# A post-norm decoder layer: the first four batches' rows are split before they are turned, and turned by DMA

## The reference, cut to what matters

```python
x = _layernorm(x + attn(x, Wq, bq, Wk, bk, Wv, bv, Wo, bo))          # first norm
x = _layernorm(x + xattn(x, ctx, ctx, mask, wq, wk, wv, wo))         # second
x = _layernorm(x + ffn(x, gate, up, down))                           # third
# _layernorm(x) = (x - mean) / sqrt(var + 1e-5), over the 512 columns
```

## Time and profile before

| | |
|---|---|
| median of three runs | 850.03 us |
| the profiled execution's own time | 849.92 us |
| its span, first to last instruction | 848.1 us |
| TensorE (PE) busy | 827.7 us, 98% |
| VectorE (DVE) busy | 689.2 us, 81% |
| GpSimd (POOL) busy | 632.8 us, 75% |
| ScalarE (ACT) busy | 533.6 us, 63% |
| mean granted TensorE clock | 0.999 of full |

### The profile page before, as it was taken

One profiled execution on the slowest core, in us unless ns is written; L12 is line 12 of the kernel. 1 busy time (PEld: TensorE's weight loads), 2 busy tenths in 40 slices (PEclk: granted clock), 3 DMA queues, 4 the chain that ended last, 5 costly groups with the idle time before them and its releaser, 6 DMA issues.

```text
span 848.1 us, 17377 instructions
## 1 busy us (share of the span) xinstructions
PE 827.7 (98%) x6125; PEld 465.5 (55%) x6125; DVE 689.2 (81%) x1077; ACT 533.6 (63%) x1560; POOL 632.8 (75%) x563
## 2 busy tenths in 40 slices
PE   9899999999999999999999999999999999999997
PEld 4677777655555554555555555555555644434444
DVE  5688788998688778689788788798889755899897
ACT  5798888554765666576575676665666753777400
POOL 1199999897676686578777677578888633999896
PEclk9999999999999999999999999999999999999999
DMA  7675255103244422434425125213442223230011
GB/s 192 194 256 181 63 160 163 54 18 108 38 95 130 112 39 75 112 39 138 105 38 155 33 40 161 38 26 91 133 93 39 46 42 105 72 110 20 2 48 52
DMA packets 120038, 76.76 MB, mean 91 GB/s; under 512 B 72877, under 2 KB 104336, under 8 KB 119952
## 3 DMA queue, kind: packets, MB, share of 16 engines
q1 hardware_dynamic: 117504, 74.86, 33.5%
q10 hardware_dynamic: 2448, 0.79, 0.5%
HBM read 52.50 MB, written 6.36 MB: 69 GB/s over the span
## 4 chain that ended last, share of the span: by engine, by line
PE 62%; POOL 14%; DVE 7%; ACT 7%; issue 6%; DMA 3%; SPq 0%; POOLq 0%; ACTq 0%; DVEq 0%
PE bank L356 16%; PE bank L358 16%; PE bank L357 16%; POOL rot L647 2%; POOL left L680 2%; PE bank L1667 2%; POOL q2l L653 2%; POOL pn L664 2%; ACT prob L845 2%; POOL prob L657 2%; PE bank L1840 1%; PE bank L1841 1%; PE bank L1760 1%; PE bank L1759 1%; PE bank L1758 1%
## 5 line engine op out<-in xcount | busy, mean ns | idle before, releaser
L657 POOL TENSOR_TENSOR prob<-prob,rden 128x512 f32<-128x512 f32 x64 | 67.8, 1060 | 103.3 <-DVE rden L1318 103.0
L647 POOL TENSOR_TENSOR rot<-rcos,rsin 128x512 f32<-128x512 f32 x80 | 106.5, 1332 | 20.3 <-DVE rsin L1260 19.8
L356 PE MATMUL bank<-aTh,xqh 128*128 128x512 f16 x256 | 97.1, 379 | 1.4 <-DVE rsin L1260 0.9
L356 PE MATMUL bank<-xoh,o2h 128*128 128x512 f16 x256 | 97.1, 379 | 0.1
L357 PE MATMUL bank<-xol,o2h 128*128 128x512 f16 x256 | 97.2, 379 | 0.0
L358 PE MATMUL bank<-xoh,o2l 128*128 128x512 f16 x256 | 97.1, 379 | 0.0
L357 PE MATMUL bank<-aTl,xqh 128*128 128x512 f16 x256 | 97.1, 379 | 0.0
L358 PE MATMUL bank<-aTh,xql 128*128 128x512 f16 x256 | 97.1, 379 | 0.0
L1010 ACT ACTIVATE prob<-bank,ebias 128x128 f32<-128x128 f32 x256 | 90.4, 365 | 2.1
L1260 DVE SCALAR_TENSOR_TENSOR rsin<-bank,sinq 64x512 f32<-64x512 f32 x128 | 88.1, 688 | 1.7
L664 POOL TENSOR_TENSOR pn<-prob,pn 128x512 f16<-128x512 f32 x64 | 84.1, 1315 | 6.8 <-ACT pn L1022 6.6
(11 more groups left out here) (224 smaller groups left out, 2652.7 us busy)
## 6 DMA issues: line engine op xcount, KB each, us to landing
tst<-tables SPq DMA_DIRECT2D x11, 768.0 KB, 5.2
xqs<-in_xwq SPq DMA_DIRECT2D x8, 1024.0 KB, 6.6
xos<-in_xwo SPq DMA_DIRECT2D x8, 1024.0 KB, 5.6
qst<-in_fq SPq DMA_DIRECT2D x11, 384.0 KB, 3.4
kstk<-stack SPq DMA_DIRECT2D x48, 64.0 KB, 2.3
qstk<-stack SPq DMA_DIRECT2D x21, 128.0 KB, 2.6
xs<-in_ctxT SPq DMA_DIRECT2D x2, 1024.0 KB, 6.3
res<-in_x SPq DMA_DIRECT2D x1, 2048.0 KB, 8.4
```

The source lines that it names most:

```text
L356: pe.matmul(out_ap, ah, bh, start=first, stop=False)
L647: nc.gpsimd.tensor_tensor(rot[:, r % 2, :], rcos[:, r % 2, :], rsin[:, r % 2, :], ALU.add).then_inc(rope_rot, 1)
L657: nc.gpsimd.tensor_tensor(prob[:, v % 2, :].rearrange("p (h k) -> p h k", h=QH), prob[:, v % 2, :].rearrange("p (h k) -> p h k", h=QH), rd ...
```

## The change

```diff
--- before.py
+++ after.py
@@ -64,9 +64,8 @@
 
 
 
-    plan = [(STEPS1 - 12, "k", (0,)), (STEPS1 - 11, "o", (0,)), (STEPS1 - 10, "o", (1,)), (STEPS1 - 9, "t", (0, 0))]
-    plan += [(STEPS1 - 9, "o", (2,)), (STEPS1 - 8, "t", (0, 1)), (STEPS1 - 8, "o", (3,)), (STEPS1 - 7, "t", (0, 2))]
-    plan += [(STEPS1 - 7, "v", (0,)), (STEPS1 - 6, "t", (0, 3))]
+    plan = [(STEPS1 - 12 + b, "o", (b,)) for b in range(BH)]
+    plan += [(STEPS1 - 8, "v", (0,)), (STEPS1 - 7, "k", (0,))]
     plan += [(STEPS1 - 5 + h, "q", (0, h)) for h in range(QH)]
     plan += [(STEPS1 - 1, "k", (1,)), (STEPS1, "v", (1,))]
     plan += [(STEPS1 + 1, "q", (1, 0)), (STEPS1 + 2, "q", (1, 1)), (STEPS1 + 3, "q", (1, 2)), (STEPS1 + 5, "q", (1, 3))]
@@ -146,7 +145,7 @@
 
 APPLY_SLOT = {(0, b): FILLS[find_fill("o", b)][0] + 1 for b in range(NB)}
 APPLY_SLOT.update({(1, b): T0 + BH * (BLOCK_OF[(G - 1, b // BH)]) + b % BH + 5 for b in range(NB)})
-SHIFTED = [(0, b) for b in range(BH, NB)]
+SHIFTED = [(0, b) for b in range(NB)]
 LATE_TURN = {APPLY_SLOT[(1, b)] + 1: b for b in range(BH, NB)}
 
 
@@ -229,7 +228,7 @@
         lnmv = sb("lnmv", [P, 3, 2], F32)
         lnve, lnrs = sb("lnve", [P, 3, 1], F32), sb("lnrs", [P, 3, 1], F32)
         power = sb("power", [P, 1], F32)
-        lnsh = sb("lnsh", [P, BH, 1], F32)
+        lnsh = sb("lnsh", [P, NB, 1], F32)
         scol16 = sb("scol16", [P, (NI - NSPLIT) * 2 * NK], F16)
         scol = sb("scol", [P, NI - NSPLIT, 2, NK], F32)
 
@@ -281,6 +280,9 @@
         o2h, o2l = at(20, "o2h", [P, 2, QH, S], F16), at(22, "o2l", [P, 2, QH, S], F16)
 
 
+        rows = at(155.5, "rows", [P, 3, 2, D], F16)
+
+
         qst = at(24, "qst", [P, 2, 3 * D], U16)
         tst = at(30, "tst", [P, 2, 2, 3 * D], F16)
         nib = at(42, "nib", [P, 3 * D], U16)
@@ -325,6 +327,7 @@
         oT_hi, oT_lo = sem("oT_hi"), sem("oT_lo")
         ln_sum, ln_stat, ln_aggr, ln_ve, ln_rs, ln_out = (
             sem("ln_sum"), sem("ln_stat"), sem("ln_aggr"), sem("ln_ve"), sem("ln_rs"), sem("ln_out"))
+        rows_hi, rows_lo, rows_in = sem("rows_hi"), sem("rows_lo"), [sem(f"rows_in{i}") for i in range(3)]
         ln_shift, ln_mid, ln_right = sem("ln_shift"), sem("ln_mid"), sem("ln_right")
         xt_hi, late_psum, late_hi, late_lo = sem("xt_hi"), sem("late_psum"), sem("late_hi"), sem("late_lo")
 
@@ -449,6 +452,13 @@
                 else:
                     sp.wait_ge(xo_lo, 4 * g)
                 sp.dma_start(xos[:, :, :], xwo.rearrange("(h p) n -> p h n", p=P)[:, g * QH:(g + 1) * QH, :]).then_inc(xo_in, 16)
+
+            def turn_rows(b):
+                if b == 0:
+                    sp.wait_ge(v1_psum, BLOCKS)
+                for i, (dst, done) in enumerate(((aTh, rows_hi), (aTl, rows_lo))):
+                    sp.wait_ge(done, b + 1)
+                    sp.dma_start_transpose(dst[:, :, b * S:(b + 1) * S], rows[:, b % 3, i, :]).then_inc(rows_in[b % 3], 16)
 
             def turn_probabilities(v):
                 sp.wait_ge(c_pn_lo, v + 1)
@@ -528,6 +538,8 @@
             load_q(1)
             stack_rows(7)
             load_kv(1)
+            for b in range(BH):
+                turn_rows(b)
             load_o(1)
             for t in range(STEPS1 - 8, END + 1):
                 if 1 <= t - T0:
@@ -723,7 +735,7 @@
 
             def inverse_sds(layer, t):
                 for (norm, b), slot in APPLY_SLOT.items():
-                    if norm == layer and slot == t + 1 and (norm, b) not in SHIFTED:
+                    if norm == layer and slot == t + 1 and (layer == 1 or slot < T0):
                         inverse_sd(layer * NB + b)
 
             for t in range(FIRST, END + 7):
@@ -833,6 +845,14 @@
                                      proj_bank(j, "v")[:, :].rearrange("p (b h d) -> p b h d", b=BH, h=HC),
                                      ACT.Copy, scale=2.0 ** (E_V1 - E_X - E_W)).then_inc(v1_hi, 1)
 
+            def split_rows_hi(b):
+                act.wait_ge(ln_out, b + 1)
+                if b == 0:
+                    act.wait_ge(v1_psum, BLOCKS - 1)
+                if b >= 3:
+                    act.wait_ge(rows_in[b % 3], 32 * (b // 3))
+                split_hi(rows[:, b % 3, 0, :], res[:, b, :], E_X).then_inc(rows_hi, 1)
+
             def exps1(u):
                 act.wait_ge(nmax_done, u + 1)
                 if u >= 2:
@@ -960,6 +980,12 @@
             for i, e in enumerate((E_QK, E_QK, E_V1)):
                 split_hi(bcols[:, i, :], bcol[:, i, :], e).then_inc(scaled_bias, 1)
             w1_split_hi(0, 2)
+            def scaled_norm(layer, b):
+                e, r = layer * NB + b, res[:, b, :]
+                act.wait_ge(ln_shift, SHIFTED.index((layer, b)) + 1)
+                nc.scalar.activation(r, r, ACT.Identity, scale=lnrs[:, e % 3, :],
+                                     bias=lnsh[:, SHIFTED.index((layer, b)), :]).then_inc(ln_out, 1)
+
             for t in range(FIRST, T0):
                 j, n = t // TILES1, t % TILES1
                 if j + 1 < BLOCKS and n == 4 and t > -TILES1:
@@ -971,6 +997,10 @@
                     seed_mask(t - STEPS1 + 2)
                 if 1 <= t <= STEPS1:
                     p1_hi(t - 1)
+                for layer, b in SHIFTED:
+                    if APPLY_SLOT[(layer, b)] == t:
+                        scaled_norm(layer, b)
+                        split_rows_hi(b)
                 if j + 2 < BLOCKS and n == 6:
                     k1_out_f32(j + 2)
                 if t == FIRST + 3:
@@ -992,12 +1022,6 @@
                 weight_pieces(t)
                 bank_splits([f for f in fills_at(t) if f not in turned_first(t)])
                 rotations(fills_at(t - 1))
-
-            def scaled_norm(layer, b):
-                e, r = layer * NB + b, res[:, b, :]
-                act.wait_ge(ln_shift, SHIFTED.index((layer, b)) + 1)
-                nc.scalar.activation(r, r, ACT.Identity, scale=lnrs[:, e % 3, :],
-                                     bias=lnsh[:, SHIFTED.index((layer, b)), :]).then_inc(ln_out, 1)
 
             def exps(v):
                 act.wait_ge(c_nmax, v + 1)
@@ -1238,6 +1262,10 @@
                 split_lo(aTl[:, :, b * S:(b + 1) * S], by_k(bank[f % 2][:, :]), aTh[:, :, b * S:(b + 1) * S],
                          E_X).then_inc(fill_free, 1)
 
+            def split_rows_lo(b):
+                dve.wait_ge(rows_hi, b + 1)
+                split_lo(rows[:, b % 3, 1, :], res[:, b, :], rows[:, b % 3, 0, :], E_X).then_inc(rows_lo, 1)
+
             def late_turned_lo(b):
                 dve.wait_ge(late_hi, b - BH + 1)
                 split_lo(aTl[:, :, b * S:(b + 1) * S], by_k(bank[4 + b % 2][:, :]), aTh[:, :, b * S:(b + 1) * S],
@@ -1457,6 +1485,9 @@
                     dve.wait_ge(table_in, 112)
                     nc.vector.tensor_scalar(mbias[:, :, :], mask_f[:, :, :], 0.0, NEG, ALU.is_equal,
                                             ALU.mult).then_inc(mask_ready, 1)
+                for b in range(BH):
+                    if APPLY_SLOT[(0, b)] == t:
+                        split_rows_lo(b)
                 weight_pieces(t - 1)
                 for f in fills_at(t):
                     if f not in turned_first(t):
@@ -1708,7 +1739,11 @@
                     if kind == "k" and n == 0:
                         pe.wait_ge(cT_lo, NHALF * NK)
                 if kind == "q":
-                    pe.wait_ge(fill_free, find_fill("t", 0, BH * ORDER[n][1] + BH - 1) + 1)
+                    if ORDER[n][1] == 0:
+                        for place in range(3):
+                            pe.wait_ge(rows_in[place], 32 * len(range(place, BH, 3)))
+                    else:
+                        pe.wait_ge(fill_free, find_fill("t", 0, NB - 1) + 1)
                     d = slice(what[1] * DK, (what[1] + 1) * DK)
                     last = project(dst[:, :], [xqh[:, i, k, d] for k in range(NK)], [xql[:, i, k, d] for k in range(NK)],
                                    aTh, aTl, cols)
```

## The result

The changed kernel takes 857.69 us, median of four runs (856.22 to 858.00), against 850.32 (848.88 to 851.07): ratio 1.0094, 95% interval 1.0079 to 1.0108. It is slower, by 7.4 us, where 6.3 were forecast. A second set of runs on another chip gave 858.77 against 850.21 and the same ratio, 1.0094 (1.0079 to 1.0109). The ratios are estimated over the undisturbed runs and are not the quotients of these medians, which are 1.0087 and 1.0101; by its medians the second set lost 8.6 us.

The account below looks back on a forecast made before the run. A loop of waits over VectorE and ScalarE, 6.6 us per turn, was taken to bound steps 54 to 56; q(0,0) 5.4 late, with GpSimd's backlog q(1,0) 6.3 late: 850.0 + 6.3 = 856.3 us, range 849.5 to 860.0.

Parts of the forecast that it names:

- The loop over VectorE and ScalarE: Steps 54 to 56: row maximum, exponentials, norm, high part, low part and consume form one turn of 6.1 to 6.6 us.
- ScalarE would do the new work in its gaps: Rival: the loop does not bind, TensorE's 3.9 us sets the step, 4.34 us won, 845.7 us; chance 0.11.
- nothing would change: In-between case: a part of the loop's cost, ending within 1.7 us of no change; chance 0.07.
- The size of the low part: VectorE's `rows_lo`: 1.1 us for batches 1 to 3 beside GpSimd's work, 0.60 for batch 0 with GpSimd idle.
- The first turn: Row maximum of step 53 at 148.2 us, GpSimd's small instructions from 153.10 before, row maximum of step 54 at 155.2.
- q(0,0): Fill after step 58 on TensorE: starts at 177.35 us, 5.4 later than 171.94.
- The transposes hid: Last transpose takes 3.1 us and lands at 176.8, before q(0,0) is otherwise free at 177.35: hidden by 0.5.
- The clock: Rival: TensorE's pauses drop the clock to half for one full step, another 3.8 us, 860.1 us; chance 0.07.
- The backlog of GpSimd: Rotation of q(0,0) 8.0 us late at 186.7, q(0,2)'s ends at 198.5; q(1,0) starts 6.3 late, through k1's bank.

Follow-up runs that it names:

- pieces_later: The changed kernel with GpSimd's six weight pieces of steps 54 to 59 moved to steps 57 to 59, two each: 863.33 us, ratio 1.0156.
- norm_back: The changed kernel with the norm of batches 0 to 3 back on VectorE, splits and DMAs kept: 852.65 us, ratio 1.0033.
- twice: The changed kernel with ScalarE making each of the four high parts twice, one after the other: 859.52 us, ratio 1.0121.
- busy: The changed kernel with 24, 8 and 34 matmuls of unread results in TensorE's pauses: 858.20 us, ratio 1.0097.
- order_only: The kernel of before with only output projections and transposes of batches 0 to 3 a step sooner, v0 and k0 behind them: 850.77 us, ratio 1.0003.
- low_swap: The changed kernel with low parts a step later on VectorE and k0 in step 56 ahead of v0 in step 57: 849.57 us, ratio 1.0002.
- low_later: The changed kernel with VectorE making each batch's low part one step later, behind that step's row maximum: 850.03 us, ratio 1.0000.
- both: The changed kernel with low parts of batches 0 to 2 a step later and GpSimd's pieces at steps 53, 54, 56 to 59: 851.25 us, ratio 1.0012.
- swap_pieces: low_swap with GpSimd's output-weight pieces of steps 60 and 61 moved to steps 66 and 68: 850.27 us, ratio 1.0006.

## Why the prediction was right, and where it was off

**The loop over VectorE and ScalarE: right, and shown.** Its turns measured 6.80, 6.82 and 5.89 against 6.6, 6.6 and 5.7. Opening it with one condition took all of the loss away. One thing the sum did not say: the loop over ScalarE alone is 6.1 to 6.2 long (`pieces_later`), and the rest is set by GpSimd, which lets the low part end. That is why 0.68 us more on ScalarE left the turn as it was. The two rivals by which the time would not grow, that ScalarE would do the new work in its gaps and that nothing would change, fall with the waits of 2.3 to 3.1 us ahead of each low part.

**The size of the low part: right in kind, low by 0.2.** 1.29 to 1.40 us where 1.1 was taken. `pieces_later` shows that GpSimd beside it makes the difference, 0.69 without. The 1.1 came from the mean of a group, 1199 ns, whose members last 0.68 to 1.79 us. What the prediction did not see is that this term depends on the others: in `norm_back` and `twice` it fell to 0.75 and 0.71 as the rest of the loop moved by 0.7 to 0.9 us.

**The first turn: 0.9 late.** The row maximum of step 53 came 5.50 us after the scores of step 52, 5.55 forecast. But GpSimd began its small instructions for batch 0 at 8.56 where the earlier trace rows gave 7.7, the difference between executions told above.

**q(0,0): forecast 34.7 us after step 52, measured 37.1.** Of the 2.4, some 0.9 is the first turn, 0.5 the low parts, and 0.9 the clock: `busy` has 35.5, and 0.7 of the 1.6 us between the two is the first turn. The transposes hid, as forecast: the last was issued at 173.82, landed 2.4 us later, and q(0,0) starts at 178.44.

**The clock: a rival that came about.** I gave it 0.07 and the price of one step at half rate, 3.8 us. It fell twice, with the pauses of 2.77 and 3.99 us, and not behind those of up to 1.02 us before the change. It cost 1.3 to 2.5 us at step 60 and 0.0 to 1.2 at step 70. The Trainium skill (TensorE: Matmul & The Clock Gate, HAM oscillation — how this bites in real kernels) says that waits for data bring the clock down and that the work behind them starts at half rate. The granted clock of the changed kernel agrees; which pause brings it down and which does not, the runs here do not settle (last section). It is not the loss's cause: with the clock full the stretch is still 7.5 us longer at step 70.

**The backlog of GpSimd: right in size, hidden in the changed kernel.** The rotation of q(0,0) was forecast at 186.7 and came at 186.75; that of q(0,2) ran from 197.25 to 198.52, forecast end 198.5. Since TensorE was later than forecast, nothing of it showed in the changed kernel: from step 63 to step 70 it takes 19.86 us, as before the change. In `busy`, where the clock is full, TensorE is 6.2 us behind at step 60 and 7.5 at step 70: the backlog's 1.3, forecast as 0.9. It reaches TensorE by another way than forecast. The wait, 1.10 us, stands in step 64 ahead of `turn1`, for exponentials behind a high part that waits for GpSimd, and not at q(1,0) behind the bank of k1.

**The total.** 7.4 by the medians of the first set, 8.6 by those of the second, against 6.3; from step 52 on the two profiles show 8.8 and 7.9. The forecast was low by more than the runs' scatter: the interval of the ratio is 6.7 to 9.2 us. What it left out is named above, the clock and the low parts for certain, GpSimd's later start in these profiles; that the first set came within 1.1 is in part luck. The profile of the first set also starts step 52 1.3 us sooner than that of before, for a cause ahead of the change that stays open.

## What to carry to other kernels

When work moves to an engine that looks half idle, write down one full turn of what each in-order queue now waits for, from an instruction back to its own successor: here 2.6 us of new work closed a loop of 6.8 around 3.9 us steps, and moving one instruction a step later opened it. Once it is open, look for what is second. In `order_only` and `low_swap` a lead of 1.2 and 1.9 us was gone to GpSimd's backlog by step 70; in `low_later` and `both` a lead of 1.3 and 0.8 us was gone to the clock by step 60. And take a price of contention from single instructions and their place, not from a group's mean.

## What the runs showed that I had not expected

- A term of contention can act as a buffer: 0.68 us more per turn on ScalarE left the turn at 6.8, since VectorE's low part ends 0.55 us after GpSimd's two-operand instruction whether it starts 0.3 or 1.0 us into it, and shrank from 1.38 to 0.71.
- The length of a pause does not tell whether the clock falls. It fell with the pause of 2.77 us ahead of v0 (0.68 of full from 162 to 166 us) and with two of 1.10 and 1.05 us in `low_later` (0.67 from 170 to 174). It did not fall with one of 2.28 us in `pieces_later` (1.00 from 204 to 212). And of the same pause ahead of q(0,0), 1.87 us in `low_swap` and 1.86 in `swap_pieces`, one left it at 1.00 from 170 to 174 us and the other saw 0.57.
- A DMA transpose of 128x512 f16 landed after 2.4 us, one of twice the size after 3.1; each of the changed kernel's holds SyncE's queue for 1.19 to 1.31 us.
- The scores of step 52 stand ahead of the first fill in which these kernels differ, and yet start anywhere from 141.3 to 144.8 us.
